# Message aggregation in three fp32r terms, behind the adjacency transposes and the gates' state parts

## What is computed

```python
# layer 3: u = adj * exp(e_n + f_m + a); h' = (u / rowsum(u)) @ h;  x = layernorm(x + h')
# layer 4, per graph, x: (512, 128)
x_conv = relu(conv17(relu(conv1(x))) + x)             # two 1-D convolutions over the nodes
s = x @ w_se.T + b_se                                  # 3 numbers a node
A = exp(-|s_n - s_m|^2) * adj                          # (512, 512)
msg = relu(x @ w_msg.T + b_msg)                        # (512, 128)
x_nmp = A @ msg                                        # the message aggregation
gi = concat(x_conv, x_nmp) @ w_ih.T + b_ih             # gates r, z, n
gh = x @ w_hh.T + b_hh
r, z = sigmoid(gi_r + gh_r), sigmoid(gi_z + gh_z)
out = (1 - z) * tanh(gi_n + r * gh_n) + z * x          # then x = layernorm(x + out)
```

## Time and profile before

| | us |
|---|---|
| median of three runs | 583.18 |
| lowest, highest | 582.69, 584.78 |
| the profiled execution | 584.18 |
| its span, first to last instruction | 582.40 |
| from turn 0's first to turn 1's first transposes of `x3` | 71.54 to 103.04 |
| an inner turn | 31.89 |
| last graph's first transposes of `x3` | 547.39 |

### The profile page before, as it was taken

How to read it: one execution, slowest core, us unless ns; L and a number is a source line. 1 busy time by engine, 2 the same in 40 slices (tenths; PEclk the granted TensorE clock), 3 DMA queues, 4 the chain that set the end, 5 groups by cost and what they waited for, 6 DMA issues and landing times.

```text
span 582.4 us, 11740 instructions
## 1 busy us (share of the span) xinstructions
PE 560.3 (96%) x3583; PEld 479.4 (82%) x3583; DVE 476.7 (82%) x1798; ACT 341.6 (59%) x713; POOL 120.8 (21%) x143
## 2 busy tenths in 40 slices
PE   6888999999999999999999999999999999999894
PEld 6767897978888797979798888979797978889684
DVE  3898777888888887888888888888888988888665
ACT  2325555575675756665756667565667566575442
POOL 3311120213122130302121211203021213122110
PEclk9989999999999999999999999999999999999998
DMA  7890050030201103030303021020303030000000
GB/s 192 277 301 4 2 191 7 2 111 2 88 22 45 64 0 109 0 109 0 109 0 109 0 52 57 17 92 0 109 0 109 0 109 1 19 2 19 1 19 18
DMA packets 33300, 34.46 MB, mean 59 GB/s; under 512 B 1663, under 2 KB 22531, under 8 KB 33146
## 3 DMA queue, kind: packets, MB, share of 16 engines
q1 hardware_dynamic: 32986, 34.01, 18.6%
q10 hardware_dynamic: 288, 0.13, 0.1%
HBM read 29.74 MB, written 4.39 MB: 59 GB/s over the span
## 4 chain that ended last, share of the span: by engine, by line
PE 85%; DVE 1%; ACT 0%; issue 0%; POOLq 0%; POOL 0%; DVEq 0%
PE bank L260 14%; PE bank L262 14%; PE bank L261 13%; PE bank L1774 9%; PE pair L260 6%; PE pair L262 6%; PE pair L261 6%; PE bank L1608 4%; PE bank L1619 3%; PE bank L1710 2%; PE pair L1766 2%; PE pair L1698 2%; PE bank L1673 1%; PE bank L1716 1%; PE pair L1725 1%
## 5 line engine op out<-in xcount | busy, mean ns | idle before, releaser
L1147 POOL TENSOR_TENSOR rs<-ve,neg_half 128x4 f32<-128x4 f32 (+1 forms) x60 | 57.1, 952 | 279.0 <-DVE ve L1336 246.2
L260 PE MATMUL bank<-cd_hi,w_hi 128*128 128x256 f32 x272 | 77.5, 285 | 0.0
L261 PE MATMUL bank<-cd_lo,w_hi 128*128 128x256 f32 x272 | 76.7, 282 | 0.0
L262 PE MATMUL bank<-cd_hi,w_lo 128*128 128x256 f32 x272 | 76.5, 281 | 0.0
L1774 PE MATMUL bank<-P,msg 128*128 128x512 f32 x128 | 57.5, 592 | 0.0
L260 PE MATMUL pair<-aT_hi,x_hi 128*128 128x512 f32 x128 | 52.9, 413 | 0.1
L260 PEld LDWEIGHTS bank<-cd_hi,w_hi 128*128 128x128 f32 x272 | 51.3, 189 | 1.6
L261 PEld LDWEIGHTS bank<-cd_lo,w_hi 128*128 128x128 f32 x272 | 51.4, 189 | 1.4
L262 PEld LDWEIGHTS bank<-cd_hi,w_lo 128*128 128x128 f32 x272 | 51.3, 189 | 0.0
L262 PE MATMUL pair<-aT_hi,x_lo 128*128 128x512 f32 x128 | 50.4, 394 | 0.0
L261 PE MATMUL pair<-aT_lo,x_hi 128*128 128x512 f32 x128 | 50.3, 393 | 0.0
(11 more groups left out here) (367 smaller groups left out, 1522.3 us busy)
## 6 DMA issues: line engine op xcount, KB each, us to landing
adj_nat<-in_adj_dram SPq DMA_DIRECT2D x16, 1024.0 KB, 6.2
x_nat<-in_x_dram SPq DMA_DIRECT2D x16, 256.0 KB, 2.9
xt<-in_x_dram SPq DMA_DIRECT2D x3, 1280.0 KB, 11.4
out_dram<-y_out SPq DMA_DIRECT2D x15, 256.0 KB, 2.2
hw<-in_L_gnn_W_dram SPq DMA_DIRECT2D x2, 640.0 KB, 6.5
xt<-in_L_gnn_conv_w_dram SPq DMA_DIRECT2D x1, 1088.0 KB, 5.8
aT<-in_adj_dram SPq DMA_DIRECT2D x5, 96.0 KB
nat_ih<-in_L_gnn_w_ih_dram SPq DMA_DIRECT2D x1, 384.0 KB, 5.1
```

The source lines that it names most:

```text
L260: nc.tensor.matmul(o, lh, rh, start=start, stop=False)
L261: nc.tensor.matmul(o, lh, rl, start=False, stop=False)
L262: return nc.tensor.matmul(o, ll, rh, start=False, stop=stop)
L1147: g.tensor_tensor(rs[i][:, 0:n], ve[i][:, 0:n], neg_half[:, 0:n], ALU.pow).then_inc(po_rs[i], 1)
```

## The change

The message aggregation is split as the others are. ScalarE rounds `msg` and each chunk of `P` (`msg_hi`, `P_hi`), VectorE writes `msg_lo`, and GpSimd, not VectorE, writes `P_lo`. TensorE adds twelve fp32r matmuls in place of four fp32 ones. It now does them behind the transposes of chunks 0 to 2 and behind the state parts of gates z and r. The other gate matmuls follow in the order `xc` of z, r, n, then `nmp` of z, r, n. On ScalarE, `y_out` goes behind the exponentials and the four roundings. On VectorE, the variance of `y3` is taken ahead of `rests_meanwhile`, and `aT_lo` of chunk 3 ahead of the second `gh` sum. In the last graph's turns, which have no adjacency to transpose, the third gate of graph 14 is done in turn 15 behind the transposes of `x3`. Buffers and semaphores are added; `three`, the taps and the first part of the program stay.

```diff
+                if cur:
+                    for mc in range(NC):
+                        wait(pool, ac_Phi[mc], V(1))
+                        wait(pool, pe_N, V(0))
+                        g.tensor_tensor(P_lo[:, mc, :], P[:, mc, :], f(P_hi[:, mc, :]), ALU.subtract).then_inc(po_Plo[mc], 1)
...
+
+                def round_weighed(mc):
+                    wait(act, dv_P[mc], V(1))
+                    wait(act, pe_N, V(0))
+                    s.activation(P_hi[:, mc, :], P[:, mc, :], ACT.Identity).then_inc(ac_Phi[mc], 1)
...
                     wait(act, dv_s, V(1))
-                    wait(act, pe_N, V(0))
+                    wait(act, dv_msglo, V(0))
...
+                    wait(act, ac_msg, V(1))
+                    wait(act, pe_N, V(0))
+                    s.activation(msg_hi[:, :], msg[:, :], ACT.Identity).then_inc(ac_msghi, 1)
...
+                if cur:
+                    round_weighed(0)
+                if nxt:
+                    wait(act, dv_e, V(2))
+                    wait(act, dv_dq, V(1))
+                    s.activation(pef[:, 0, :], ef[:, 0, :], ACT.Exp, bias=c12[:, 0:1]).then_inc(ac_pe, 1)
+                if nxt:
+                    wait(act, pe_agg2, V(2))
+                    s.activation(agg_sb[:, :], AG_BANK[:, :], ACT.Identity).then_inc(ac_agg2, 1)
+                if cur:
+                    exponential(2)
+                    exponential(3)
+                    round_weighed(1)
+                    round_weighed(2)
+                    round_weighed(3)
                 if prev and cur:
...
-                if nxt:
-                    wait(act, dv_e, V(2))
-                    wait(act, dv_dq, V(1))
-                    s.activation(pef[:, 0, :], ef[:, 0, :], ACT.Exp, bias=c12[:, 0:1]).then_inc(ac_pe, 1)
-                if nxt:
-                    wait(act, pe_agg2, V(2))
-                    s.activation(agg_sb[:, :], AG_BANK[:, :], ACT.Identity).then_inc(ac_agg2, 1)
-                if cur:
-                    exponential(2)
-                    exponential(3)
+                if cur:
...
                 def weigh(mc):
                     wait(dve, ac_E[mc], V(1))
-                    wait(dve, pe_N, V(0))
+                    wait(dve, po_Plo[mc], V(0))
                     v.tensor_tensor(P[:, mc, :], AT_BANK[mc % 2][:, :], aT[par][:, mc, :], ALU.mult
                                     ).then_inc(dv_P[mc], 1)
...
+                def rest_of_state():
+                    wait(dve, ac_x3T, V(1))
+                    wait(dve, pe_r, V(0))
+                    v.tensor_tensor(x3T_lo[:, :], X_BANK[:, :], f(x3T_hi[:, :]), ALU.subtract).then_inc(dv_x3Tlo, 1)
+
+                if prev:
+                    if nxt:
+                        split_rest(3, 2)
+                    else:
+                        rest_of_state()
                     wait(dve, dv_t0, V(0))
                     wait(dve, pe_gn, V(0))
                     v.tensor_tensor(gh, SQ_BANK[:, :], gh, ALU.add).then_inc(dv_t, 1)
-                if nxt and prev:
-                    split_rest(3, 2)
-                if cur:
-                    wait(dve, ac_x3T, V(1))
-                    wait(dve, pe_r, V(0))
-                    v.tensor_tensor(x3T_lo[:, :], X_BANK[:, :], f(x3T_hi[:, :]), ALU.subtract).then_inc(dv_x3Tlo, 1)
+                if nxt and cur:
+                    rest_of_state()
                     if not prev:
                         finish_first_part()
...
+                if cur:
+                    wait(dve, ac_msghi, V(1))
+                    wait(dve, pe_N, V(0))
+                    v.tensor_tensor(msg_lo[:, :], msg[:, :], f(msg_hi[:, :]), ALU.subtract).then_inc(dv_msglo, 1)
...
                 if nxt:
                     hold(dve, dv_y3, V(2))
-                    statistics(2, V, 2, lambda c: y3[:, c, :], EPS, rests_meanwhile)
-                else:
-                    rests_meanwhile()
+                    statistics(2, V, 2, lambda c: y3[:, c, :], EPS)
+                rests_meanwhile()
...
+                if cur and not nxt:
+                    gate(SQ_BANK[:, :], of_inputs(2), pe_gn, 0)
...
-                if cur:
-                    wait(pe, ac_msg, V(1))
-                    if prev:
-                        wait(pe, ac_out, V(0))
-                    for mc in range(NC):
-                        wait(pe, dv_P[mc], V(1))
-                        last = t_.matmul(X_BANK[:, :], msg[:, ch(mc)], P[:, mc, :], start=(mc == 0), stop=(mc == NC - 1))
-                    last.then_inc(pe_N, 1)
+                def gate_part(o, blk, hi, lo, start, stop):
+                    return three(pe, o, w_hi[:, blk, :], w_lo[:, blk, :], hi[:, :], lo[:, :], start, stop)
+
                 if new:
                     wait(pe, adj_in[par], dma(2))
                     for mc in range(2):
                         wait(pe, dv_P[mc + 2], V(1))
                         transpose_adjacency(mc)
+                if cur and nxt:
+                    wait(pe, ac_msg, V(1))
+                    gate_part(MS_BANK[:, :], HH + 1, x3T_hi, x3T_lo, True, False)
+                    wait(pe, dv_conv, V(1))
+                    gate_part(CV_BANK[:, :], HH, x3T_hi, x3T_lo, True, False)
+                if new:
                     wait(pe, dv_conv, V(1))
                     transpose_adjacency(2)
+                if cur:
+                    if prev:
+                        wait(pe, ac_out, V(0))
+                    wait(pe, dv_msglo, V(1))
+                    for mc in range(NC):
+                        wait(pe, ac_Phi[mc], V(1))
+                        t_.matmul(X_BANK[:, :], msg_hi[:, ch(mc)], P_hi[:, mc, :], start=(mc == 0), stop=False)
+                        t_.matmul(X_BANK[:, :], msg_lo[:, ch(mc)], P_hi[:, mc, :], start=False, stop=False)
+                    for mc in range(NC):
+                        wait(pe, po_Plo[mc], V(1))
+                        last = t_.matmul(X_BANK[:, :], msg_hi[:, ch(mc)], P_lo[:, mc, :], start=False, stop=(mc == NC - 1))
+                    last.then_inc(pe_N, 1)
                 if cur and nxt:
                     wait(pe, dv_xclo, V(1))
-                    gate(MS_BANK[:, :], of_state(1) + of_inputs(1), pe_z, 1)
+                    gate_part(MS_BANK[:, :], IH + 2, xc_hi, xc_lo, False, False)
+                    gate_part(CV_BANK[:, :], IH, xc_hi, xc_lo, False, False)
+                if cur and new:
+                    wait(pe, dv_y3, V(2))
+                    gate_part(SQ_BANK[:, :], IH + 4, xc_hi, xc_lo, True, False)
                 if cur and nxt:
-                    gate(CV_BANK[:, :], of_state(0) + of_inputs(0), pe_r, 1)
-                    wait(pe, dv_y3, V(2))
-                    gate(SQ_BANK[:, :], of_inputs(2), pe_gn, 1)
+                    wait(pe, dv_nmplo, V(1))
+                    gate_part(MS_BANK[:, :], IH + 3, nmp_hi, nmp_lo, False, True).then_inc(pe_z, 1)
+                    gate_part(CV_BANK[:, :], IH + 1, nmp_hi, nmp_lo, False, True).then_inc(pe_r, 1)
+                if cur and new:
+                    gate_part(SQ_BANK[:, :], IH + 5, nmp_hi, nmp_lo, False, True).then_inc(pe_gn, 1)
                 if new:
                     wait(pe, dv_aTlo[0], V(3))
                     transpose_adjacency(3)
```

23 lines of the change are left out of this document (14 added, 9 removed).

## The result

The changed kernel takes 589.83 us (median of 4 runs, 589.37 to 591.22) where the kernel before, run beside it on the same chip, takes 583.58: a ratio of 1.011, 95% interval 1.0078 to 1.0143. That is 6.25 us slower; the forecast was 9.2 slower. The profiled execution took 590.29 around a span of 588.6, so the two spans differ by 6.2.

The account below looks back on a forecast made before the run. The prediction took one loop, VectorE and TensorE taking turns, to bound the 31.89 us turn. Over 14 steps, 0.44 each gave +6.2, the ends +3.0: 9.2 slower, 592.4 us forecast, range 581 to 602.

Parts of the forecast that it names:

- TensorE's own sum: TensorE's message sum: twelve fp32r matmuls (2.78) and kind changes (0.11) replace 3.44 us, 0.55 less a turn.
- T: Start of TensorE's last adjacency transposes in a turn, 15.23 us after the second aggregation's start in the kernel before.
- N from S + 8.51 to S + 10.84: Message sum's end, counted from the second aggregation's start in TensorE's turn: claimed to come 2.33 us later.
- The string behind N: VectorE's work from the message sum's end to the third gate's sum: 7.36 us, making the third tanh 0.44 later.
- I find no slack in this chain: From third tanh to the next second aggregation: the 0.44 delay passes in full, turn 32.33 us instead of 31.89.
- The loop as first described: Turn of 31.89: second aggregation's start to last adjacency transposes 15.23, to `x3T_lo` end 3.43, VectorE to next aggregation 13.23.
- GpSimd at 1.10: Each of GpSimd's four `P_lo` subtractions takes 1.10 us, no cost a turn; at 1.30, 0.3 to 0.4 longer.
- `msg_lo` above 1.0, meeting the second `P_lo`: VectorE's `msg_lo`, starting at 252.42, is held by GpSimd's subtraction and ends near 253.65, without cost.
- The small `dq` product: VectorE's tiny product in the statistics: not held by GpSimd, no cost; by the skill's sentence, +1 us in the sum.
- The ends: Last graph's part: bank wait +2.5, filled idle -0.5 to -1.0, lower clock 0 to +2.5; +3.0 taken.
- TensorE stays the limit: Rival for the turn: VectorE follows easily, turn 31.52 us, 0.37 less, 581.0 in all; turn shorter, chance 0.15.
- Both sides meet: Rival for the turn: unseen slack soaks up the tanh's 0.44, only the ends cost, 586 us; chance 0.12.

Follow-up runs that it names:

- before_swap: Kernel before, with VectorE's fourth `aT_lo` (chunk 3) put ahead of the `gh` sum; 588.0 us, ratio 1.0069 to the kernel before.
- fp32_late: Changed kernel's order, but the message sum in four fp32 matmuls, without rounding, `msg_lo` and `P_lo`; 595.3 us, ratio 1.0199 to the kernel before.
- before_rest3_pool: Kernel before, with the fourth `aT_lo` of a turn subtracted by GpSimd instead of VectorE; 590.8 us, ratio 1.0101 to the kernel before.
- rest3_pool: Changed kernel, with the fourth `aT_lo` of a turn subtracted by GpSimd instead of VectorE; 588.8 us, ratio 1.0082 to the kernel before.
- plo_short: Changed kernel, with GpSimd's four `P_lo` subtractions cut from 512 columns to 4; 591.6 us, ratio 1.0137 to the kernel before.
- xlo_early: Changed kernel, with VectorE's `x_lo` of the inputs moved between the first and second `aT_lo`; 587.4 us, ratio 1.0059 to the kernel before.
- swap_back: Changed kernel, with VectorE's fourth `aT_lo` put back behind the `gh` sum; 593.1 us, ratio 1.0154 to the kernel before.
- tail_split: Changed kernel, with the output between the second and third rounding in the last graph's turn alone; 589.4 us, ratio 1.0098 to the kernel before.

## Why the prediction was right, and where not

- *TensorE's own sum.* Twelve matmuls and a change of kind for four fp32 ones: the sum runs 255.22 to 258.10, 2.88 with its first one, where 2.78 and 0.08 were forecast. Right. T is only 0.40 earlier than before, since some 0.13 went at the second transpose, as said.
- *N from S + 8.51 to S + 10.84.* S + 10.79. Right.
- *The string behind N.* `nmp_lo` was forecast at N + 0.67 and came at N + 0.75; the tanh at S + 18.23, and came at S + 18.16, released by VectorE. Right to 0.07.
- *"I find no slack in this chain".* This step failed. It had 0.21: 0.15 where `c1` waited for conv1 and 0.06 where x waited for w0. The 0.44 of the forecast should have been 0.44 - 0.21 = 0.23, and was 0.17: +2.4 over 14 turns in place of +6.2. Of the missing 3.8, 2.9 is this one term (14 x 0.21), the rest the tanh's 0.07. The earlier trace rows showed `co_lo` waiting for `co_hi`, and I followed the wait to ScalarE's queue but not to what ScalarE had waited for. before_swap and fp32_late show the slack as such, at two further doses.
- *The loop as first described.* S to T to E to S: E to S is not one VectorE stretch, x waits for TensorE there. before_rest3_pool shows it: 0.33 more on TensorE's way to conv1 moved x by as much, and the turn by 0.45. The terms of the sum didn't rest on it, the verdict "no slack" did.
- *GpSimd at 1.10.* Mis-sized: 1.48 on average beside a working VectorE (group below), 1.30 for one alone in rest3_pool. The cost was still 0, since the cover held at `nmp_lo` within 0.08 and ScalarE's copy hid that; plo_short shows 0. I expected the 1.30 case to cost 0.3 to 0.4 a turn, so that reasoning was wrong too, in the safe direction.

```profile
L1186 POOL TENSOR_TENSOR P_lo<-P,P_hi 128x512 fp32r<-128x512 f32 x64 | 93.4, 1481 | 48.3 <-ACT P_hi L1211 48.3
```

- *`msg_lo` above 1.0, meeting the second `P_lo`.* Right: 1.37, ending at 254.55, that is S + 7.07, where 253.65 in the trace of before, S + 6.93, was said. It waits for the second `P_lo` (252.72 to 254.00) and then does its 0.55. The third `P_lo`, next in GpSimd's queue, starts at 253.96 and takes 1.74: it is held by `msg_lo` in its turn.
- *The small `dq` product.* I went by the `s_sq` row and expected 0.16; it took 0.78, in all 15 turns, and 0.16 in plo_short. The row misled me: a root of four columns beside it is not a subtraction of 512. The Trainium skill, page SBUF — State Buffer, section "Who interferes with whom", says that the engine that issues second is blocked for the whole instruction of the first, and the trace agrees here (0.78 against 0.16), while beside the root `s_sq` wasn't held; what makes the root different isn't shown. The microsecond that the prediction derived from that rule didn't come all the same, since ScalarE's copies cover what was lost.
- *The ends.* Forecast +3.0 (between +1 and +5), measured +3.9. The later start was sized right, 3.33 (3.2 by the prediction's times 564.81 and 568.0), and so nearly was the shorter sum, 0.5 where 0.7 was said. The stretch at the lower clock, to which I gave 0 to 2.5, came in the changed kernel's trace and cost 1.5; in rest3_pool's it didn't come. Wrong in kind was the gain from the moved gate: the lower stretch at 551 is gone (it had cost 1.2), but the gate's new place costs 0.7. That leaves a gain of 0.45, and a loss of 0.7 where that stretch doesn't come.
- *The rivals.* "TensorE stays the limit" fell by the changed kernel itself. "Both sides meet" was half true: 0.21 of the tanh's delay was soaked up, about half. With the loss in the turns at 2.4 the result lies between that rival (586) and the forecast. The range and "slower" held, partly by luck: two terms erred in opposite directions, the turns by 3.8 and the ends by 0.9, and whether the clock falls in the last turn moves the time by another 1.5.

What stays open: why two turns in a row differ by 0.05 to 0.1 in all kernels but before_rest3_pool, and what decides whether the clock falls behind a wait of the same length and for how long (not at all in rest3_pool's trace, 3.4 us in the changed kernel's, 6.8 in those of xlo_early and swap_back).

## What to carry to other kernels

Where an engine waits, follow the wait through its releaser to what that one waited for; a chain has no slack only when each link was shown to wait for the one before it. A step that is moved to where its engine has time moves its result as well: ask who consumes it last in the turn, and price the move by that, not by the engine's own sum. A form that pays in a full turn may cost in the last one, where its preparation stands open; keep the old form there. Before a difference at a program's end is put down to the edit, look at the granted clock there, in more than one trace.

## What the hardware showed

- A VectorE step with two inputs in SBUF, or a `tensor_scalar` from SBUF to SBUF, is held until a running GpSimd subtraction of 128x512 has ended, whatever the step's own size: a 128x4 product took 0.78 in place of 0.16, a 128x128 normalisation 1.33 in place of 0.34, a 128x512 subtraction 1.37 in place of 0.68. Not held were steps with one operand in PSUM (`gh` at 0.68 beside 1.30 of GpSimd) and a 128x4 reciprocal (0.18 at 254.72, inside `P_lo`). By the same page and section of the Trainium skill a step with at most one SBUF input doesn't contend, with the exception of the faster forms of operations like `tensor_scalar`. The rows fit both halves; in which form the normalisation ran they don't show.
- The price goes both ways: GpSimd's 128x512 subtraction takes 1.30 alone (rest3_pool), and up to 1.75 between VectorE's (changed kernel).
- TensorE's clock can fall to the 1.2 GHz level in a wait or behind it, and the same wait in the same place can leave it at 2.4 GHz. Behind 1.95 us it fell in the traces of before and before_swap and not in before_rest3_pool. Behind 2.15 it fell (tail_split), behind 3.14 to 3.18 in six traces and not in a seventh (rest3_pool), and not behind 1.62 (fp32_late). The cost in the message sum was 1.5 us for a stretch of 3.4 us and 2.4 us for one of 6.8 us.
